# Reciprocals of the softmax sums by way of DRAM and a broadcast DMA instead of a matmul, in a fused attention and expert kernel

## The reference

```python
xn = layernorm(layernorm(x), g1, b1)                  # attention half
q  = (xn @ Wq) in 16 heads of 64;  k, v = split(xn @ Wkv)   # one k and v for all heads
attn = softmax(q k^T * 64**-0.5)                      # 512 x 512 for each head
x1 = x + layernorm(concat_heads(attn @ v) @ Wo, g2, b2)
h  = layernorm(x1)                                    # expert half
p  = softmax(h @ gate_w.T);  two best of 8 experts, their weights scaled to sum 1
out = x1 + sum over the two: w_e * ((up_e(h) * gelu(gate_e(h))) @ down_e.T)
```

## Time and profile before

| | |
|---|---|
| Runs | 617.56, 619.30, 623.29 us; median 619.3 |
| The profiled execution | 618.97 us, of which the span from first to last instruction is 617.2 |
| TensorE matmuls busy | 574.6 us (93%) |
| VectorE, GpSimd busy | 400.0 us (65%), 393.6 us (64%) |
| ScalarE busy | 297.7 us (48%) |
| Mean granted TensorE clock | 0.977 |
| DMA | 29.46 MB, mean 48 GB/s |

### The profile page before, as it was taken

How to read it: one execution, slowest core, us unless ns; L and a number is a source line. 1 busy time by engine, 2 the same in 40 slices (tenths; PEclk the granted TensorE clock), 3 DMA queues, 4 the chain that set the end, 5 groups by cost and what they waited for, 6 DMA issues and landing times. The chain is left out here.

```text
span 617.2 us, 8768 instructions
## 1 busy us (share of the span) xinstructions
PE 574.6 (93%) x2543; PEld 326.6 (53%) x2543; DVE 400.0 (65%) x861; ACT 297.7 (48%) x559; POOL 393.6 (64%) x329
## 2 busy tenths in 40 slices
PE   8899999999999998989999989999997988999990
PEld 6555454444554453445545444444433577888880
DVE  4887657567655869763676977974665666444433
ACT  2245645356446454552655445365436553455540
POOL 6357677567669755796795569869638834354330
PEclk9799999999999999998999999999998998999996
DMA  5111012011010200080000000000007200230005
GB/s 163 69 71 70 33 40 72 1 70 46 28 71 1 72 2 1 9 299 5 2 4 1 1 6 21 13 2 4 10 0 193 52 23 29 69 88 28 22 15 204
DMA packets 27373, 29.46 MB, mean 48 GB/s; under 512 B 7715, under 2 KB 18469, under 8 KB 27328
## 3 DMA queue, kind: packets, MB, share of 16 engines
q1 hardware_dynamic: 25056, 24.66, 12.5%
q0 software_dynamic: 2272, 4.24, 2.1%
HBM read 13.50 MB, written 15.32 MB: 47 GB/s over the span
## 5 line engine op out<-in xcount | busy, mean ns | idle before, releaser
L1139 ACT ACTIVATE prob<-s_ps 128x512 f32<-128x512 f32 x256 | 150.9, 600 | 191.0 <-PE s_ps L1236 188.9
L1059 DVE TENSOR_REDUCE less_max<-max_ps 128x1 fp32r<-128x512 f32 x256 | 173.6, 688 | 85.2 <-PE max_ps L1214 82.5
L985 POOL TENSOR_TENSOR fold<-prob 128x1024 f32<-128x1024 f32 x63 | 149.7, 2376 | 92.9 <-ACT prob L1139 92.4
L1250 PE MATMUL pv_ps<-prob,v 128*64 128x512 f32 x512 | 138.1, 619 | 0.0
L1234 PE MATMUL s_ps<-q_hl,khh 128*128 128x512 f32 x256 | 118.2, 462 | 0.7 <-ACT prob L1139 0.7
L1214 PE MATMUL max_ps<-khh,q_hl 128*128 128x512 f32 x256 | 104.0, 410 | 8.9 <-DVE less_max L1059 5.8
L1236 PE MATMUL s_ps<-q_hm,kly 65*128 65x512 f32 x256 | 102.1, 399 | 0.0
L1234 PEld LDWEIGHTS s_ps<-q_hl,khh 128*128 128x128 f32 x256 | 48.6, 190 | 85.7 <-ACT prob L1139 67.1
L991 POOL TENSOR_TENSOR psums<-fold 128x512 f32<-128x512 f32 x63 | 80.8, 1282 | 4.9
L1214 PEld LDWEIGHTS max_ps<-khh,q_hl 128*128 128x128 f32 x256 | 49.1, 192 | 30.4 <-DVE less_max L1059 12.1
L1236 PEld LDWEIGHTS s_ps<-q_hm,kly 65*128 65x128 f32 x256 | 48.8, 191 | 9.0 <-issue 3.3
(11 more groups left out here) (226 smaller groups left out, 758.9 us busy)
## 6 DMA issues: line engine op xcount, KB each, us to landing
sorted_rows<-raw_w SPq DMA_DIRECT2D x36, 260.0 KB, 2.6
raw_w<-in_gate_upT SPq DMA_DIRECT2D x8, 512.0 KB, 8.9
wd<-in_downT SPq DMA_DIRECT2D x8, 256.0 KB
raw_w<-parts SPq DMA_DIRECT2D x8, 256.0 KB, 4.1
psums<-sorted_rows SPq DMA_DIRECT2D x22, 65.0 KB
x<-in_x SPq DMA_DIRECT2D x4, 256.0 KB, 4.6
out<-x SPq DMA_DIRECT2D x4, 256.0 KB, 2.5
xs_first<-sorted_rows SPq DMA_DIRECT2D x15, 65.0 KB, 1.9
```

What stands on the lines that cost most here:

```text
L985: nc.gpsimd.tensor_tensor(fold[:, :, :], prob[:, head % 4, 0:2, :], prob[:, head % 4, 2:4, :], ALU.add).then_inc(prob_folded, 1)
L1059: nc.vector.tensor_reduce(less_max[:, group % 2, col:col + 1], max_ps[:, k % 2, :], AX_X, ALU.max, negate=True).then_inc(max_done, 1)
L1139: nc.scalar.activation(prob[:, head % 4, jt, :], s_ps[:, k % 2, :], ACT.Exp, scale=SCALE).then_inc(exp_done, 1)
L1250: last = nc.tensor.matmul(pv_ps[DH * hd:DH * hd + DH, :], v[:, b % 2, jt, :], prob[:, head % 4, jt, :], start=(jt == 0), stop=(jt == JT - 1))
```

## The change

The reciprocals (one per head and query) no longer become float32r halves, and `headsel`, `rhl` and the NORM matmul are gone, with their loads and GpSimd preparation at the start. RECIP is now one VectorE instruction. GATHER writes `rinv` to the DRAM tensor `recips` (one DMA of 16 KB). A new step CAST, at tail slot 11 behind that slot's SHIFT, waits for it and reads it back by two DMAs into `over_sum`, each to 64 partitions x 4 x 512 (512 KB each). NORM is then `ao = over_sum * raw`, both in SBUF, at tail slots 17, 19, 21, 23 (before: 14, 17, 19, 22); OUT follows 4 slots behind (before: 5). FILL stands behind CAST. The input steps APPLY0, XT and XL of a batch come one slot earlier; XSTAT is moved; CHOOSE5 is split into CHOOSE5, 6 and 7 at separate slots; the LIST steps are spread wider. The handover's order is rewritten.

```diff
-IN_AT = (5, 14, 18, 18, 21, 22, 25, 26)
-AFTER_AT = (29, 30, 33, 43, 51, 52, 54, 54, 55, 57, 58, 60, 63, 67, 69, 82, 84, 86, 88)
-LATE_AFTER_AT = (29, 30, 33, 41, 45, 47, 48, 48, 49, 50, 52, 53, 54, 55, 56, 58, 59, 60, 61)
+IN_AT = (5, 13, 17, 17, 21, 22, 25, 26)
+AFTER_AT = (29, 30, 33, 45, 51, 52, 54, 54, 55, 57, 58, 60, 61, 63, 65, 67, 69, 84, 88, 92, 95)
+LATE_AFTER_AT = (29, 30, 33, 40, 45, 47, 48, 48, 49, 50, 52, 53, 54, 54.5, 55, 55, 56, 58, 59, 60, 61)
-NORM_AT = (14, 17, 19, 22)
-OUT_LAG = 5
+NORM_AT = (17, 19, 21, 23)
+OUT_LAG = 4
+CAST_AT = 11
...
         place(at, 3, "SHIFT", n, 0)
+        place(at, 6, "FILL", n, 0)
...
+            place(after + CAST_AT, 5, "CAST", u, 0)
...
             if kind == "CHOOSE5":
                 link(dve, nc.vector.tensor_tensor(of_pick[:, :, :, :], pick[:, :, :, :], ...
+            if kind == "CHOOSE6":
                 link(dve, nc.vector.tensor_reduce(share[:, :, :], of_pick[:, :, :, :], AX_X, ALU.add))
                 link(dve, nc.vector.tensor_tensor(most[:, :], share[:, 0, :], share[:, 1, :], ALU.add))
+            if kind == "CHOOSE7":
                 link(dve, nc.vector.reciprocal(over[:, :], most[:, :]))
...
             if kind == "RECIP":
                 dve.wait_ge(spread_in, 32 * (u + 1))
-                link(dve, nc.vector.reciprocal(rinv[:, :], spread[:, :]))
                 if u >= 1:
-                    dve.wait_ge(rhl_in, 32 * u)
-                link(dve, nc.vector.tensor_copy(halves[:, 0, :], rinv[:, :]))
-                nc.vector.tensor_tensor(halves[:, 1, :], rinv[:, :], halves[:, 0, :].bitcast(F32),
-                                        ALU.subtract).then_inc(recip_done, 1)
+                    dve.wait_ge(recips_out, 16 * u)
+                nc.vector.reciprocal(rinv[:, :], spread[:, :]).then_inc(recip_done, 1)
             if kind == "NORM":
-                dve.wait_ge(norm_mm, k + 1)
+                dve.wait_ge(over_sum_in, 32 * (u + 1))
...
-                nc.vector.tensor_tensor(ao[:, k % 2, :], sum_ps[:, :], raw[:, k % RAW_SLOTS, :],
+                nc.vector.tensor_tensor(ao[:, k % 2, :], over_sum[:, a, :], raw[:, k % RAW_SLOTS, :],
...
             if kind == "GATHER":
                 sp.wait_ge(recip_done, u + 1)
+                sp.dma_start(recips[u].rearrange("(p c) -> p c", c=SPREAD), rinv[:, :]).then_inc(recips_out, 16)
+            if kind == "CAST":
+                sp.wait_ge(recips_out, 16 * (u + 1))
                 if u >= 1:
-                    sp.wait_ge(norm_mm, u * UP)
-                else:
-                    sp.wait_ge(consts_set, 1)
-                for part in range(2):
-                    sp.dma_start(rhl[part * LOW_ROW:part * LOW_ROW + UH, :].bitcast(F32),
-                                 halves[:, part, :].bitcast(F32)).then_inc(rhl_in, 16)
+                    sp.wait_ge(ao_ready, u * UP)
+                of_heads = recips[u].rearrange("(c h q) -> h c q", h=2, q=S)
+                for hd in range(2):
+                    sp.dma_start(over_sum[DH * hd:DH * hd + DH, :, :],
+                                 of_heads[hd].unsqueeze(0).broadcast_to([DH, UP, S])).then_inc(over_sum_in, 16)
...
-            if kind == "NORM":
-                k = u * UP + a
-                pe.wait_ge(rhl_in, 32 * (u + 1))
-                if k >= 1:
-                    pe.wait_ge(ao_ready, k)
-                nc.tensor.matmul(sum_ps[:, :], headsel[:, a, :], rhl[:, :], start=True,
-                                 stop=True).then_inc(norm_mm, 1)
...
                 tail_sync(sp, "SPREAD", last_unit)
+                load_down(0)
+                load_down(1)
+                load_rows(sp, EARLY_ROWS, rows(EARLY_ROWS))
+                tail_sync(sp, "GATHER", last_unit)
+                for e in range(2, E):
+                    load_down(e)
+                tail_sync(sp, "CAST", last_unit)
...
                 low_gate_up(dve, 1, wl_ready)
-                tail_vector(dve, "NORM", last_unit, 0)
                 low_gate_up(dve, 2, wl_ready)
-                tail_vector(dve, "NORM", last_unit, 1)
                 hidden(1)
-                tail_vector(dve, "NORM", last_unit, 2)
-                tail_vector(dve, "NORM", last_unit, 3)
+                for c in range(UP):
+                    tail_vector(dve, "NORM", last_unit, c)
                 hidden(2)
...
                 turn_in(2)
-                tail_tensor(pe, "NORM", last_unit, 0)
                 gate(2)
-                tail_tensor(pe, "NORM", last_unit, 1)
-                tail_tensor(pe, "OUT", last_unit, 0)
-                tail_tensor(pe, "NORM", last_unit, 2)
+                up(2)
                 turn_hidden(0)
-                tail_tensor(pe, "OUT", last_unit, 1)
-                tail_tensor(pe, "NORM", last_unit, 3)
-                up(2)
-                tail_tensor(pe, "OUT", last_unit, 2)
-                tail_tensor(pe, "OUT", last_unit, 3)
+                for c in range(UP):
+                    tail_tensor(pe, "OUT", last_unit, c)
                 turn_hidden(1)
```

More of the change, by code:

```diff
@@ L78, in attention_schedule @@
     for n, (head, _) in enumerate(shifts(units)):
-        place(FIRST_SHIFT_AT[n] if n < 2 else JT * head - lead + 1, 3, "SHIFT", n, 0)
+        at = FIRST_SHIFT_AT[n] if n < 2 else JT * head - lead + 1
+        place(at, 3, "SHIFT", n, 0)
+        place(at, 6, "FILL", n, 0)
     for u in range(units):
@@ L278, in bass_preln_mqa_moe_kernel @@
         rinv = sb(whole, "rinv", [P, SPREAD])
-        halves = sb(whole, "halves", [P, 2, SPREAD], F32R)
-        rhl = sb(whole, "rhl", [P, S], F32R)
+        over_sum = sb(whole, "over_sum", [P, UP, S])
         raw = sb(whole, "raw", [P, RAW_SLOTS, S])
@@ L811, in bass_preln_mqa_moe_kernel @@
         last_pv = max(n for n, step in enumerate(steps) if step[0] == "PV")
-        tail_steps = [step for step in steps[last_pv:] if step[0] in ("RAW", *RECIP_STEPS, "NORM", "OUT")]
+        tail_steps = [step for step in steps[last_pv:] if step[0] in ("RAW", *RECIP_STEPS, "CAST", "NORM", "OUT")]
         assert all(step in tail_steps or step[0] in ("PV", "SUM") for step in steps[last_pv:])
@@ L878, in _ @@
                 sp.dma_start(wof[:, :, :], wo.rearrange("(c p) n -> p c n", p=P)).then_inc(wo_in, 16)
-                for half in range(2):
-                    for part in range(2):
-                        row = part * LOW_ROW + half * UH // 2
-                        sp.dma_start(hs_raw[row:row + UH // 2, :, :],
-                                     head_rows[half + 2 * part:P:32, :, :]).then_inc(hs_in, 16)
                 for b in range(1, NB):
@@ L967, in _ @@
                         if k == 0:
-                            link_pool(pool, nc.gpsimd.memset(headsel[:, :, :].bitcast(F32), 0.0))
-                            link_pool(pool, nc.gpsimd.memset(rhl[:, :].bitcast(F32), 0.0))
-                            pool.wait_ge(hs_in, 64)
-                            for part in range(2):
-                                held = slice(part * LOW_ROW, part * LOW_ROW + UH)
-                                nc.gpsimd.tensor_scalar(headsel[held, :, :], hs_raw[held, :, :], 1.0, 1.0, ALU.mult,
-                                                        ALU.mult).then_inc(headsel_set, 1)
-                                pool.wait_ge(headsel_set, part + 1)
                             set_constants(pool)
@@ L1612, in up, with keep_busy @@
                     times(up_ps[:, k % 2, :], k, F).then_inc(up_mm, 1)
-                def keep_busy(times):
-                    for _ in range(times):
-                        nc.tensor.matmul(ht_ps[:, :], headsel[:, 0, :], headsel[:, :, :].rearrange("p k c -> p (k c)"),
-                                         start=True, stop=True)
-                keep_busy(4)
+                def keep_busy(width):
+                    nc.tensor.matmul(ht_ps[:, 0:width], ident[:, :], wof[:, 0:width // P, :].rearrange("p k c -> p (k c)"),
+                                     start=True, stop=True)
+                keep_busy(S)
                 turn_in(0)
-                keep_busy(2)
+                keep_busy(S // 2)
                 for e in range(E):
```

37 lines of the change are left out of this document (16 added, 21 removed).

## The result

The changed kernel took 634.26 us (median of 4 runs, 632.89 to 635.03) beside 620.47 of the kernel before on the same chip: a ratio of 1.022, 95% interval 1.0166 to 1.0274. Run again with the later experiments, on a chip where the kernel before took 617.1, its ratio was 1.0241 (1.022 to 1.0262). So it is slower by over 2%, outside the range of 610 to 625 us. The second figure is the tighter one, and the experiments are compared with it; 0.01 of a ratio is 6.2 us. TensorE has 34 matmuls less (2543, now 2509): the 32 that were forecast, and two in `keep_busy` (six before, four now), which the prediction didn't count.

A forecast was written before the change was run, and what follows sets the result against it. TensorE's issue was taken as the bound. The terms -6.4 + 2.9 - 5.0 - 0.7 + 3.2 + 4.6 = -1.4 us, from 618.97, gave 617.6; the forecast was 617.5 us, range 610 to 625.

The forecast's parts named there:

- The NORM matmuls and OUT's slots: Attention tails: 28 removed matmuls at 0.23 us, 6.4 us less; OUT's new slots between float32r matmuls, 2.9 us more.
- The routing steps: Tails: CHOOSE5 split, XSTAT and a LIST step moved, 5.0 us of TensorE's waits on VectorE go; XL's slot 0.7 more.
- XL's: TensorE's 2.86 us wait on XL: one slot earlier takes 0.7 us off, bounds 0 and 2.9.
- The lock's rule: NORM's product: a VectorE instruction with two SBUF inputs waits for a GpSimd instruction reading SBUF, under an exclusive lock.
- The two DMA legs ... Cost 0.: GATHER's write and CAST's read back: landed at 107.0, before VectorE's call at 107.43 in a tail, so no cost.
- The prediction's deciding point: CAST's landing at 108.7, 7.5 us behind the second issue, from which the late landing would hold VectorE.
- the slow rival: Second rival: over_sum lands late at NORM 0, TensorE loses 1.2 us in each of seven tails; +9.9, 629 us; chance 0.13.
- The sentence on the Trainium skill: CAST: 64 partitions reach half the DMA ports, 196 GB/s, 5.4 us for both halves; the landing moves to 109.
- NORM's new operands ... 3.2.: Attention tails: products wait for GpSimd's operations, the next reduction is late at slot 22; 7 x 0.45 = 3.2 us more.
- The clock falls to 0.50 behind the shorter wait already; I count no difference.: Handover: the longer wait before the last unit's OUTs adds no cost through the clock.
- The last unit ... 4.6 us more.: Handover: CAST behind six wd loads lands about 478, four NORMs take 6.0; last OUT at 484.9 against 480.26.
- rival 3: Attention saves, but the handover gives it back (+8.3) with attention stalls of 6: +5, 624 us; chance 0.15.

The follow-up runs named there:

- e4: Kernel before with only the routing part (CHOOSE5 in three steps, new IN and AFTER slots), NORM still a matmul: 0.9865, 611.9 us.
- e3: Changed kernel; in seven attention units the product reads a constant SBUF tile and doesn't wait for CAST's landing, DMAs kept: 1.0124.
- e14: Changed kernel run again without an edit, beside later experiments: 1.0241.
- e15: Changed kernel with FILL placed eight slots later; the edit didn't reach the queue, so in effect the changed kernel again: 1.0252.
- e2: Changed kernel; in seven attention units the product reads sum_ps (PSUM) in place of over_sum, wait for the landing kept: 1.0106.
- e11: Kernel before with the routing part alone, plus the attention units' product reading a constant SBUF tile in place of sum_ps: 0.9937.
- e10: Changed kernel with nine unused float32 matmuls filling TensorE's wait before the last unit's first OUT: 1.0238.
- e13: Changed kernel with five unused float32 matmuls filling TensorE's wait before RANK of the batch before the last: 1.0172.
- e1: Changed kernel with the last unit's CAST issued right behind GATHER, ahead of the six wd loads: 1.0151, 628.7 us.
- e5: Changed kernel; in seven attention units the product reads sum_ps (PSUM) and waits for no landing, DMAs and last unit kept: 1.0005.
- e8: Changed kernel with CAST as four DMAs, one per pair of heads over 128 partitions, in place of two over 64: 1.0904, 675.9 us.

## Why the prediction was wrong, step by step

**What held.** The NORM matmuls and OUT's slots: 2.2 us over six tails once lock and landing are away, forecast 3.0. The routing steps: -8.3 us, forecast -5.7; in e4 the waits went nearly as named, and XL's came back with the path. The lock's rule: a product of two SBUF operands that meets GpSimd's work waits for it, one with PSUM doesn't (28 of 28), as the Trainium skill says (SBUF — State Buffer, Who interferes with whom). Its size where nothing is late, 4.5 us, was near the 3.2, and the four products of the last unit took 6.1 us from the first's start to the last's end, forecast 6.0.

**"The two DMA legs ... Cost 0."** This step failed, but not where it was worked out. I took the 5.8 us of a 512 KB load behind the second issue; the landing came 7.3 us behind it in unit 0's tail and 6.9 in unit 4's, and cost 7.3 us by e3's ratio. The prediction's deciding point was 108.7, 7.5 us behind the second issue. In the changed kernel VectorE and GpSimd come to this place 1.2 us later, so the point moves to 109.9, and the landing only just reached it: TensorE waited 0.20 us in that tail, and as much in e3 with no landing to wait for. What costs is the landing elsewhere: just behind the start of a `fold`, 2.4 us each time (e14 and e15), and in unit 5's tail, where the LIST steps queue behind it (4.5 us of waits, 2.1 without). So the slow rival was right that the landing would be late, and near the size with its 8.4 us in attention. It was wrong that TensorE would lose 1.2 us in each of seven tails. It had a chance of 0.13. The sentence on the Trainium skill gave 109 (SBUF — State Buffer, Door 1: The DMA port swizzle). The trace is nearer to it than to my row: 215 and 216 GB/s in unit 4's tail, with nothing beside CAST, where it says 196. That the 64 partitions are the reason, no run here shows.

**"NORM's new operands ... 3.2."** The rule was right, the place was not. I worked it out in unit 0's tail, which has no routing steps, and multiplied by seven. There I looked at who waits for the next maxima behind NORM: in the first five tails TensorE lost 0 to 0.6 us on them. In the tail of unit 6 the late product and the held steps beside it push `picked` to `upto` from one `fold` to the next, and RANK waits on the last of them: 5.4 us with the lock on the product, 1.0 without (e2). The lock cost 8.4 us in the changed kernel, RANK's wait and clock included. That is more than e11's 4.5, but the two intervals overlap. The products took 1.14 us in the mean, not the 1.6 to 2 that I named.

**"The clock falls to 0.50 behind the shorter wait already; I count no difference."** It was said of the handover, and there it held (e10). I had put the clock at nothing in attention without a look: it cost 4.3 us behind RANK (e13).

**"The last unit ... 4.6 us more."** It was 8.6. The products had their size; the landing had not. It was forecast 14.9 us behind the SPREAD and came at 18.4, and e1 shows the loads of `wd` ahead of it as the larger part: 5.2 of the 8.6 us come back with the order changed, and the landing then comes 13.7 us behind the SPREAD. Against e4, which has the new routing and the old handover, the last OUT is not 8.6 but 10.7 us later.

**The sum.** With the measured sizes: routing -8.3 (e4); lock and landing together +14.6 (e5); what is left of the path, +8.7 (e5 above e4). That is +15.0; it must close, since the three are differences in one chain of ratios, and 13.8 to 15 were measured. The +8.7 is the handover: 10.8 us in the profiles of e5 and e4, less 1.5 by which what follows is shorter in e5's. The matmuls and OUT's slots, forecast at -3.5, leave nothing at the last SPREAD. The forecast had -5.7, +3.2, +4.6 and -3.5 in these places. Rivals 2 and 3 of the prediction, the late landing and the handover that gives it all back, both came true in the same kernel, in size if not in each place; I had priced them as alternatives. A slip of the prediction: a third of rival 3's 0.15 is 0.05, not 0.04, so slower by over 1% had 0.18.

## What to carry to other kernels

Price a wait on TensorE together with the clock behind it: where TensorE is the bound, a wait of 5.4 us came with 7 us at half clock in some executions and with 13 to 14 in others, and in the latter cost twice its length. Where a new step on VectorE becomes slower or later, follow every chain that is queued behind it, not just the nearest, and ask which operation of GpSimd each will then meet. Don't work out one tail and multiply by seven: the tail of unit 0 showed almost nothing, and the cost came in the tails that also carry routing steps. A landing near its deciding point is a cost with a chance, not zero, and causes that don't exclude each other are to be added. The version to keep is e4, the smaller routing steps without the path through DRAM.

## What the runs showed of the hardware that was not expected

A DMA to 128 partitions whose outermost dimension is 2 ran at 47 to 51 GB/s and a DMA share of 0.13, and its four issues held SyncE 9.46 us (e8). To 64 partitions with an outermost dimension of 64 the same bytes ran at 215 and 216 GB/s, and an issue took 0.67. Not only products of 128x512 are held: `taken`, a TENSOR_SCALAR of 128x8, took 2.71 us and ended with a `fold`. It had started 0.3 us before that `fold`, but GpSimd was then in one of SEND's indirect DMAs, from 384.82 to 385.79. A product that started 0.33 us ahead of a `fold`, with GpSimd idle, took 0.69. The clock stayed at 0.50 for 7 us in three executions and for 13 to 14 in four, from inside a wait of 5.0 to 5.4 us on, with TensorE busy behind it in all of them. And the same kernel's units differ from one execution to the next by some 2 to 4 us, by whether a landing falls just before a `fold` or just behind its start, and by how long the clock stays low; that would explain why its intervals are wide.
